# Output projections of three sequences as three float32r products of high and low halves (one Trainium2 core)

## What is computed

```python
h = _rmsnorm(x, pre_norm_w)
a = jax.nn.sigmoid(h @ w_a + decay_bias)
i_gate = jax.nn.sigmoid(h @ w_i)
v = h @ w_v
input_signal = jnp.sqrt(jnp.clip(1.0 - a * a, 1e-08)) * (i_gate * v)
rec_out = _chunked_scan(a, input_signal)
x = x + rec_out @ out_proj_w          # the product that the change rewrites
h2 = _rmsnorm(x, ffn_norm_w)
gate, up = jnp.split(h2 @ w_gate_up, 2, axis=-1)
return x + jax.nn.silu(gate) * up @ w_down
```

## Time and profile before

| | |
|---|---|
| Runs before | 337.16, 335.62, 336.93 us; median 336.93 us |
| The profiled execution | 337.17 us, with a span of 335.4 us from first to last instruction |
| PE busy | 294.9 us, 88% of the span |
| PEld busy | 259.9 us, 77% |
| DVE busy | 205.3 us, 61% |
| ACT busy | 168.7 us, 50% |
| POOL busy | 158.5 us, 47% |
| Mean granted TensorE clock | 0.958 of full speed |

### The profile page before, as it was taken

The page is one execution under the profiler, slowest core; times in us unless marked ns, Lnnn a source line. Parts: engine busy times, 40 slices in busy tenths (PEclk is TensorE's granted clock), DMA queues, the critical chain, the costliest instruction groups (busy, mean ns, idle before and its releaser), DMA issues.

```text
span 335.4 us, 5642 instructions
## 1 busy us (share of the span) xinstructions
PE 294.9 (88%) x1842; PEld 259.9 (77%) x1842; DVE 205.3 (61%) x466; ACT 168.7 (50%) x353; POOL 158.5 (47%) x130
## 2 busy tenths in 40 slices
PE   6499996696592898979899998999999998999994
PEld 5488895475481787868798997889899787888883
DVE  2478838969989685548945545884665552343333
ACT  3679438559373143574436457543655753222220
POOL 5423006602407144667855866687586664407000
PEclk9779999879699599999999999999999999999999
DMA  7999920005013002323333344334344544939941
GB/s 220 352 385 364 412 73 0 0 2 188 0 17 119 19 21 45 62 54 57 66 62 57 63 75 72 49 64 81 50 69 76 66 50 47 142 48 138 211 155 63
DMA packets 31228, 34.29 MB, mean 102 GB/s; under 512 B 5088, under 2 KB 28896, under 8 KB 31168
## 3 DMA queue, kind: packets, MB, share of 16 engines
q0 software_dynamic: 11712, 14.58, 27.6%
q1 hardware_dynamic: 16560, 17.25, 15.0%
q10 hardware_dynamic: 2928, 2.10, 1.9%
HBM read 22.06 MB, written 13.96 MB: 107 GB/s over the span
## 4 chain that ended last, share of the span: by engine, by line
PE 69%; DVE 15%; ACT 7%; issue 4%; DMA 2%; POOL 1%; SPq 1%; DVEq 0%; ACTq 0%
PE ps L352 57%; PE ps L548 4%; PE ps L412 4%; PE ps L378 2%; DMA X<-in_L_attn_x_dram 2%; DVE Wpj_lo L1056 1%; ACT h L704 1%; DVE Wfc_lo L1056 1%; DVE guT_lo L1066 1%; ACT gain L692 1%; DVE gu L1061 1%; ACT Wfc_hi L643 1%; DVE both L964 1%; DVE tmp L956 1%; PE ps L361 1%
## 5 line engine op out<-in xcount | busy, mean ns | idle before, releaser
L1273 POOL DMA_INDIRECT xg<-xh_dram,gather_u x39 | 51.2, 1312 | 60.7 <-DVE picks L1091 30.6
L1282 POOL DMA_INDIRECT acc_dram<-yb,gather_u x39 | 62.4, 1600 | 15.3 <-issue 7.9
L352 PE MATMUL ps<-Wd_hi,guT_hi 128*128 128x256 f32 x128 | 37.1, 290 | 7.4 <-DVE guT_lo L1066 7.4
L352 PE MATMUL ps<-h2T_lo,Wgu_hi 128*128 128x512 f32 x128 | 43.5, 401 | 0.0
L352 PE MATMUL ps<-h2T_hi,Wgu_hi 128*128 128x512 f32 x128 | 41.4, 405 | 1.1 <-DVE h2T_lo L938 1.1
L1061 DVE TENSOR_TENSOR gu<-gu,ps 128x512 f32<-128x512 f32 x32 | 21.9, 684 | 31.7 <-PE ps L352 30.5
L352 PE MATMUL ps<-h2T_hi,Wgu_lo 128*128 128x512 f32 x128 | 40.2, 395 | 0.0
L352 PE MATMUL ps<-Wd_hi,guT_lo 128*128 128x256 f32 x128 | 37.0, 289 | 0.0
L352 PE MATMUL ps<-Wd_lo,guT_hi 128*128 128x256 f32 x128 | 37.0, 289 | 0.0
L735 ACT ACTIVATE guT_hi<-gu 128x512 fp32r<-128x512 f32 x32 | 20.1, 629 | 27.9 <-DVE gu L1061 27.9
L726 ACT ACTIVATE gu<-ps 128x512 f32<-128x512 f32 x32 | 19.1, 596 | 29.7 <-PE ps L352 29.7
(11 more groups left out here) (167 smaller groups left out, 683.5 us busy)
## 6 DMA issues: line engine op xcount, KB each, us to landing
X<-acc_dram POOLq DMA_DIRECT2D x8, 512.0 KB, 9.8
acc_dram<-zero SPq DMA_DIRECT2D x1, 2176.0 KB, 14.4
X<-in_L_attn_x_dram SPq DMA_DIRECT2D x4, 512.0 KB, 6.7
Wgu_raw<-in_L_attn_w_gate_up_dram SPq DMA_DIRECT2D x4, 512.0 KB, 10.4
xh_dram<-X ACTq DMA_DIRECT2D x4, 512.0 KB, 8.2
Wfc_raw<-in_L_ffn_w_fc_dram SPq DMA_DIRECT2D x4, 512.0 KB, 11.9
Wpj_raw<-in_L_ffn_w_proj_dram SPq DMA_DIRECT2D x4, 512.0 KB, 4.1
out_dram<-X SPq DMA_DIRECT2D x3, 512.0 KB, 5.8
```

Of the source, the lines that this page charges most:

```text
L352: return nc.tensor.matmul(dst, lhs, rhs, start=start, stop=stop, skip_group_check=group)
L1273: pool.indirect_dma_start(out=xg[i % XG][:, :], out_offset=None, in_=xh_dram, in_offset=bass.IndirectOffsetOnAxis(ap=gather_u[:, i:i + 1], ...
L1282: pool.indirect_dma_start(out=acc_dram[i % 2], in_=yb[i % YB][:, :], in_offset=None, compute_op=ALU.add, out_offset=bass.IndirectOffsetOnA ...
```

## The change

The projections of sequences 1, 2 and 3 are computed as three float32r products of halves; sequence 0 stays as it was.

- `out_proj_w` is split once: ScalarE writes `Wo_hi` (a Copy, 128x512) after the last expert weight's high half, and VectorE writes `Wo_lo` (a subtraction, 128x512) at the end of the second block of step 4. `Wo_hi` lies over constants that are no longer read then, so ScalarE waits for the routing's end (`routed`, `experts_ready`), and VectorE for the projection of sequence 0 (`o_done`).
- The recurrence is split for each of the three sequences at the end of the second block of step 5, 9 or 15: ScalarE makes two Copies of 128x512 into `rec_hi` (one for each `r`, each waiting for its scan), VectorE two subtractions of 128x512 into `rec_lo`. `rec_hi` lies where `gi[b]` was, `rec_lo` is written over `dec[b]`.
- PE waits, before side 0, for both subtractions of the sequence (`rec_split`) and for `Wo_lo` (`wo_split`). A side (256 tokens) was 4 float32 matmuls of 256 columns and becomes 12 float32r matmuls of 256 columns.

```diff
+        Wo_hi, Wo_lo = put("Wo_hi", [P, K, D], F32R, routing_at), put("Wo_lo", [P, K, D], F32R, top[0] - 2 * KB)
...
+        rec_hi = [put(f"rec{b}_hi", [P, K, S], F32R, slot_at[b % 3] + 4 * KB) for b in range(B)]
+        rec_lo = [put(f"rec{b}_lo", [P, K, S], F32R, slot_at[b % 3]) for b in range(B)]
...
                         pe.wait_ge(*[(gu_ready, d + 1) for d in PROJECT if PROJECT[d] == b][0])
+                    if b:
+                        pe.wait_ge(rec_split, K * b)
+                        pe.wait_ge(wo_split, 1)
                 for j in (2 * side, 2 * side + 1):
-                    for k in range(K):
-                        last = nc.tensor.matmul(ps[:, side, (j % 2) * D:(j % 2 + 1) * D],
-                                                dec[b][:, k, j * P:(j + 1) * P], Wo[:, k, :], start=k == 0, stop=k == K - 1)
+                    to, toks = ps[:, side, (j % 2) * D:(j % 2 + 1) * D], slice(j * P, (j + 1) * P)
+                    if b == 0:
+                        for k in range(K):
+                            last = nc.tensor.matmul(to, dec[b][:, k, toks], Wo[:, k, :], start=k == 0, stop=k == K - 1)
+                    else:
+                        for n, (l, h) in enumerate(PRODUCTS):
+                            for k in range(K):
+                                last = product(to, (rec_hi, rec_lo)[l][b][:, k, toks], (Wo_hi, Wo_lo)[h][:, k, :],
+                                               n + k == 0, n == 2 and k == K - 1)
                 last.then_inc(o_done, 1)
...
+            def split_wo():
+                act.wait_ge(wo_loaded, 16)
+                act.wait_ge(routed, 1)
+                act.wait_ge(experts_ready, 1)
+                A.activation(Wo_hi[:, :, :], Wo[:, :, :], ACT.Copy).then_inc(wo_hi, 1)
+
+            def split_rec(b):
+
+                for r in range(K):
+                    act.wait_ge(rec_ready, K * b + r + 1)
+                    A.activation(rec_hi[b][:, r, :], dec[b][:, r, :], ACT.Copy).then_inc(rec_is_hi, 1)
...
             weights_hi(ALL - 1)
+            split_wo()
...
+                        if v == 1 and d in PROJECT:
+                            split_rec(PROJECT[d])
...
+            def split_wo():
+                dve.wait_ge(wo_hi, 1)
+                dve.wait_ge(o_done, 2)
+                V.tensor_tensor(Wo_lo[:, :, :], Wo[:, :, :], Wo_hi[:, :, :].bitcast(F32), ALU.subtract).then_inc(wo_split, 1)
+
+            def split_rec(b):
+                for r in range(K):
+                    dve.wait_ge(rec_is_hi, K * (b - 1) + r + 1)
+                    V.tensor_tensor(rec_lo[b][:, r, :], dec[b][:, r, :], rec_hi[b][:, r, :].bitcast(F32),
+                                    ALU.subtract).then_inc(rec_split, 1)
...
+                        if d == FIRST and v == 1:
+                            split_wo()
+                        if v == 1 and d in PROJECT:
+                            split_rec(PROJECT[d])
```

More of the change, by code:

```diff
@@ L89, in recurrent_moe_block @@
         pre_w, ffn_w, bias = put("pre_w", [P, K]), put("ffn_w", [P, K]), put("bias", [P, K])
-        ident, ones = put("ident", [P, P]), put("ones", [P, P])
+        ident = put("ident", [P, P])
+        routing_at = top[0]
+        ones = put("ones", [P, P])
         before, ones_bf = put("before", [P, P], BF16), put("ones_bf", [P, P], BF16)
+        lane_i, lane = put("lane_i", [P, P], I32), put("lane", [P, P])
+        lane16 = put("lane16", [P, P], F16)
+        assert top[0] >= routing_at + 2 * KB
         one = put("one", [P, 1])
         half, minus_half = put("half", [P, T]), put("minus_half", [P, T])
-        lane_i, lane = put("lane_i", [P, P], I32), put("lane", [P, P])
         lane_p, row_of = put("lane_p", [P, 1]), put("row_of", [P, NB + 1])
-        lane16 = put("lane16", [P, P], F16)
         token_i, token = put("token_i", [P, T], I32), put("token", [P, T])
@@ L213, in recurrent_moe_block @@
                                                              sem("signal_ready"), sem("rec_ready"))
+        wo_hi, wo_split, rec_is_hi, rec_split = sem("wo_hi"), sem("wo_split"), sem("rec_is_hi"), sem("rec_split")
         o_done, x1_done, ssq_ready, rn2_ready = sem("o_done"), sem("x1_done"), sem("ssq_ready"), sem("rn2_ready")
```

## The result

The changed kernel took 342.93 us (median of 6, 340.06 to 345.99) against 337.52 us (335.62 to 340.68) for the kernel before beside it: a ratio of 1.0153, 95% interval 1.0114 to 1.0191. It is slower, as forecast, but by 5.4 us and not by 2.56, and outside the range of 337.5 to 341.0. That the two series differ this much is part of the answer: 1.5 us of it is the changed kernel's median, 1.1 us that of the kernel before. Medians here are over all executions of a kernel; ratios and intervals leave out those more than 1.5% above its fastest.

A forecast was written before the change was run, and what follows sets the result against it. PE, busy 88% of the span with 69% of the chain, was taken to bound the kernel. Terms -1.68 + 1.11 + 1.11 + 1.38 + 0.64 = +2.56 us gave a median of 339.5 us, range 337.5 to 341.0.

The forecast's parts named there:

- The products: Projections on PE: 12 products per side at 0.12 us, 1.44 us; 0.28 us shorter per side, 1.68 us over six.
- weight loads: Rival at the projections: loads do not hide behind products, a side takes 3.72 us, total 353.2 us; chance 0.02.
- The splits of sequences 2 and 3: Copies and subtractions ahead of these projections: PE starts 1.00 us later, plus 0.11 exposed weight load, +1.11 us each.
- a sign: Ahead of sequences 2 and 3, PE waiting about 1.1 us for the subtraction would show the forecast right.
- `Wo_lo`: Weight's low half on VectorE in step 4 delays the third block's expert layer: +0.64 us, bounds 0 and 0.69.
- The wait of sequence 1: PE's wait ahead of sequence 1's projection, already 1.22 us, grows by its split: PE starts 1.38 us later.
- The sum without a fall: Whole kernel: -1.68 + 1.11 + 1.11 + 1.38 + 0.64 = +2.56 us, with no clock fall included.
- the prediction's range: Median of the whole kernel: 337.5 to 341.0 us, the high end taking four splits 0.3 us dearer plus scatter.
- The clock: Rival at sequence 1's projection: PE idle grows from 1.2 to 2.6 us, clock halves, 2.9 us lost, 342.4; chance 0.03.
- 2.13 us of wait at 144.21 left the clock whole: Argument against the clock rival, from PE's wait for normalised sequence 1 in the profile before the change.

The follow-up runs named there:

- the two series: Two measurements of the same changed kernel against the kernel before: 342.93 against 337.52 us (ratio 1.0153), then e11, 341.44 against 338.59 us (1.0078).
- e6: Changed kernel with `Wo_lo` written earlier, in the first block of step 4 ahead of the square: 341.36 us, ratio 1.0092 to the kernel before.
- e3: Kernel before plus only sequence 1's copies and subtractions, results unused, and PE's wait for them; projections stay float32: 341.84 us, ratio 1.0091.
- e11: Changed kernel measured again, unchanged, for a second profile and more executions: 341.44 us against 338.59 for the kernel before, ratio 1.0078.
- e9: Changed kernel with thrown-away products in both long PE waits of sequence 1, 12 ahead of its projection, 8 ahead of its transposes: 341.08 against 338.59 us, ratio 1.0110.
- e2: Change for sequences 2 and 3 alone, sequence 1 in float32, `Wo_lo` written in step 6: 339.46 us, ratio 1.0040 to the kernel before.
- e4: As e2, but the splits of sequences 2 and 3 stand a block earlier: 338.78 us, ratio 1.0020 to the kernel before.
- e1: Changed kernel with 11 thrown-away products ahead of sequence 1's projection, placed behind the old scan wait: 341.87 us, ratio 1.0102 to the kernel before.
- e5: Changed kernel with 12 thrown-away products ahead of PE's first wait for sequence 1's projection: 341.63 us, ratio 1.0120 to the kernel before.
- e7: Kernel before with thrown-away products in four PE waits, its three longest and the one of 2.13 us: 336.48 against 338.11 us, ratio 0.9937.
- e8: e7's fillers plus sequences 2 and 3 split a block early, `Wo_lo` in step 6's first block, sequence 1 in float32: 335.61 us, ratio 0.9908 to the kernel before.
- e10: Kernel before with 8 thrown-away products in the 2.1 us wait ahead of sequence 1's transposes: 338.52 us, ratio 1.0019.

## Why the prediction was wrong, point by point

**The products: right.** Side 1 of sequence 2 runs from 183.24 to the transpose at 184.66, 1.42 us; the sum had 1.44.

```profile
183.24 0.40 PE L361 MATMUL ps<-Wo_hi,rec_hi 128*128 128x256 f32 x2
...
184.66 0.38 PE L566 MATMUL ps<-ident,xg 128*128 128x128 f32 x2
```

The spacing by the Trainium skill (TensorE: Matmul & The Clock Gate, Back-to-back issue gap), which the section gives for an isolated matmul, would have made it 1.31 us, an estimate; the trace is with the `Wd` rows. The Trainium skill's sentence on weight loads (same page, The mechanism), that a load overlaps running matmuls only when its row group differs, would have kept twelve loads from hiding here; the trace shows the opposite: a new 128x128 weight for each product, and 0.12 us from one to the next. (The same section also names a background weight buffer into which a load is pulled ahead; no run here tells what these loads used.)

**The splits of sequences 2 and 3: right.** The rows of sequence 2:

```profile
178.32 0.39 ACT L793 ACTIVATE act_e<-ps 128x256 f32<-128x256 f32 x1 [0.33 <-PE ps L361]
...
178.60 1.14 ACT L723 ACTIVATE rec_hi<-dec 128x512 fp32r<-128x512 f32 x2
...
179.26 1.29 DVE L967 TENSOR_TENSOR rec_lo<-dec,rec_hi 128x512 fp32r<-128x512 f32 x2
...
180.47 0.42 DVE L1143 TENSOR_TENSOR xgT_lo<-ps,xgT_hi 128x256 fp32r<-128x256 f32 x1
```

The relu starts 5.86 us later than in the earlier trace rows, the projection 6.90: a delay of 1.04 us, forecast 1.00. Some of that closeness is luck: the last subtraction ended 1.84 us behind the relu and not 2.01, but PE started 0.26 us behind the subtraction and not 0.05. The whole step, wait less shorter sides, was 0.51 and 0.50 us in the table, forecast 1.11 - 0.56 = 0.55. PE's idle time ahead of the projections was 0.87 us, where 1.1 had been named as a sign.

**`Wo_lo`: right, a little less.** 0.43 us in the table and 0.54 by e6, against 0.64; `Wo_hi` ran in ScalarE's idle time and cost nothing.

**The wait of sequence 1: right, a little more.** 1.59 us against 1.38. The last subtraction ends at 130.66 + 1.47 = 132.13 and the first product starts at 132.39; it takes PE 0.26 us to get going there, not the 0.05 of the old rows, and this is the whole difference. In e3, where float32 products stand behind the same wait, it was 0.15 (132.38 to 132.53). Why the three differ is not shown.

**The sum without a fall: right.** 0.43 + 1.59 + (15.04 - 15.70) + 0.51 + 0.50 + 0.04 = 2.4 us, taking the stretch behind the projection from e11; forecast 2.56. e9, with both waits filled, is 2.4 us over the kernel before in its profile and 2.5 by the medians. A slip in the prediction's range changes nothing of this: four splits 0.3 us dearer and half a microsecond of scatter on 339.5 make 341.2, not 341.0.

**The clock: the step that failed.** The miss is 3.4 us (342.93 against 339.5). Of it 0.6 us is the base, since the kernel before came out at 337.52 and not at 336.93; the other 2.8 us is what the sum left out. In the profile that is the clock: from the first expert layer to the last product it took 225.84 us against 220.77, 5.07 more. By e11's stretch of 15.04 without a fall they split into the 2.41 of the sum above and 2.66 for the fall behind the projection's wait. The sum had this fall at nothing. The prediction had the mechanism and the price among its rivals (2.9 us, 342.4) and gave it a chance of 0.03, on the argument that "2.13 us of wait at 144.21 left the clock whole". That was one execution. The profiles, taken together ("after" is the first profile of the changed kernel):

| Wait on PE, from 120 us on | half clock behind it | no half clock |
|---|---|---|
| 2.7 to 2.8 us, projection of sequence 1 | after, e3, e6 | e11 |
| 2.6 us, transposes of sequence 1 | | e2, e4 |
| 2.13 to 2.15 us, transposes of sequence 1 | e1, e5, e6, e11 | before, after, e3 |
| 0.9 and 1.2 us, projections | | all that have them |

The wait of 2.8 us is new with the change. So a wait of this length has a chance of a fall, and one execution without it gives no bound. What a fall costs goes by how long half clock lasts. For 6.8 us it was 17.70 - 15.04 = 2.66 us (profile after). For 3.4 us it was 1.4 (e6, 16.48 - 15.04) and 1.6 (e3) behind the projection's wait, and 0.7 to 0.9 behind that for the transposes (e1, e5, e6 and e11 against 59.97). The first series also had luck against it: its profiled execution drew the long fall, lost 1.86 us ahead of the change as well, and its median is 1.5 us above that of e11. By the pairs of medians the change cost 5.4 us in one series and 2.9 in the other.

The Trainium skill (TensorE: Matmul & The Clock Gate, What's actually happening) says that the chip's look at TensorE's activity is "free-running", it does not begin anew with the kernel; e11 against the profile after is in line with it, the same wait with and without a fall, and does not prove it. The prediction left that sentence out of account. Its range should have reached to the sum plus a fall, 342 us, with the measurement's scatter on top.

**Left open.** Which share of executions falls at which wait was not counted; a profile shows one execution of each run, and the mean clock of the others does not say where they fell. That filling removes a fall is shown at the two waits ahead of 115 us, where half clock stands in every other profile and in neither e7 nor e8. At the waits of 2.8 and 2.1 us, behind which it comes only in some executions, the filled profiles (e1, e5, e9, e10) have none, which agrees but is too few to prove it. That the falls make up the rest of the time in the medians is not shown: e9 is 2.5 us over the kernel before by the medians but 3.7 by its ratio of 1.0110, e11 with nothing filled 2.9 and 2.6, and the two cannot be told apart.

## What to carry to other kernels

A split that must run between a producer and TensorE has a fixed length (here 1.14 us of copies, then the last subtraction), and it is won or lost by where it stands in the two in-order queues: one block earlier turned a loss of 0.5 us per sequence into a gain of 0.6 in the traces. When a change lengthens a wait on TensorE to 2.1 us, the shortest behind which the clock fell here, or more, put the price of a clock fall into the main case with a chance of its own, and look at several executions before calling a wait harmless. Where PE must wait anyway, products that are thrown away in the wait can be cheaper than the wait, but only in stretches that PE itself bounds.

## What the runs showed of the hardware

- From 120 us on, waits on TensorE of 2.13 to 2.81 us were followed by half clock in seven cases and not in six, with both outcomes for the same code; the waits of 0.9 and 1.2 us never were in the profiles here.
- Between 120 us and the last product, half clock lasted 3.4 us six times and 6.8 us once, and cost 0.7 to 2.7 us. The 6.8 us behind the wait at 88 us cost nothing, since something else set the pace there.
- float32r products of 256 columns with a new weight each came every 0.12 us; a float32 one took 0.43 us in its place.
- From the end of what it waited for to its first product TensorE took 0.05 us (the scan, float32), 0.15 us (e3, a subtraction, float32) and 0.26 us (a subtraction, float32r).
